# A causal mask added by TensorE's products, maximum and subtraction from the banks, and steps moved between phases

## The reference

```python
h = patches @ W + b + pos ;  h = concat([cls_tok, h])              # 32 images x 26 tokens
h = h + attn1(layernorm(h))                                       # causal
y = layernorm(h)
    # attn2: rms_norm(y) * norm1_w, qkv, rope, then
    scores = where(tril, q @ k.T / sqrt(64), finfo.min); attn = softmax(scores)
    x2 = y + attn @ v @ w_out
    # experts: two of 16 by top_k of softmax(rms_norm(x2) @ w_router)
    out = x2 + sum_e combine[:, e] * ((silu(gate) * up) @ w_down[e])
return h + out
```

## Time and profile before

| | us |
|---|---|
| median of 3 runs | 337.66 (336.48 to 338.42) |
| profiled execution | 340.81 |
| its span, first to last instruction | 338.9 |
| busy: TensorE, weight loads | 274.5, 232.9 |
| busy: VectorE, GpSimd, ScalarE | 149.4, 123.8, 91.5 |
| mean granted clock of TensorE | 0.934 |

### The profile page before, as it was taken

The page is one execution under the profiler, slowest core; times in us unless marked ns, Lnnn a source line. Parts: engine busy times, 40 slices in busy tenths (PEclk is TensorE's granted clock), DMA queues, the critical chain, the costliest instruction groups (busy, mean ns, idle before and its releaser), DMA issues.

```text
span 338.9 us, 5708 instructions
## 1 busy us (share of the span) xinstructions
PE 274.5 (81%) x1917; PEld 232.9 (69%) x1917; DVE 149.4 (44%) x347; ACT 91.5 (27%) x248; POOL 123.8 (37%) x138
## 2 busy tenths in 40 slices
PE   1999889979889999698999779803899999999900
PEld 0988779868768889487998669703677776777600
DVE  0143845764744568733867843570022222222204
ACT  1016640204532216512100532100233333333200
POOL 5030002573001291011794056063334523666640
PEclk9999999959999999999999999755899999999965
DMA  7301992004500007000000000392111596222226
GB/s 297 156 2 43 390 314 71 2 0 140 140 0 21 0 2 186 2 5 17 1 2 0 3 1 21 96 343 76 37 35 39 163 281 169 72 70 58 62 72 219
DMA packets 16641, 30.56 MB, mean 90 GB/s; under 512 B 6500, under 2 KB 10820, under 8 KB 15780
## 3 DMA queue, kind: packets, MB, share of 16 engines
q1 hardware_dynamic: 11140, 20.43, 20.1%
q0 software_dynamic: 2720, 4.55, 4.8%
q10 hardware_dynamic: 2752, 5.18, 4.5%
HBM read 26.07 MB, written 4.09 MB: 89 GB/s over the span
## 4 chain that ended last, share of the span: by engine, by line
PE 31%; DVE 21%; issue 16%; POOL 14%; DMA 11%; ACT 6%; SPq 0%; POOLq 0%; DVEq 0%; ACTq 0%
PE bank L1228 8%; POOL front L596 4%; POOL slots L580 4%; DMA experts<-wgu 4%; POOL parts L602 3%; PE bank L1244 3%; PE bank L1286 2%; PE bank L1333 2%; POOL rstd_a L516 2%; PE bank L1112 2%; DVE experts L835 2%; DMA front<-fw 2%; DVE experts L951 2%; DMA front<-moe_in,probs_by_key 2%; DVE experts L829 2%
## 5 line engine op out<-in xcount | busy, mean ns | idle before, releaser
L1100 PE MATMUL bank<-constants 128*128 128x96 f32 x376 | 48.4, 289 | 15.3 <-DMA slots<-slot_contents,slot_index 15.3
L1100 PEld LDWEIGHTS bank<-constants 128*128 128x128 f32 x376 | 47.1, 205 | 16.0 <-DMA slots<-slot_contents,slot_index 15.5
L1333 PE MATMUL bank<-experts,probs_by_key 96*128 x152 | 52.3, 487 | 0.6 <-ACT probs_by_key L758 0.6
L596 POOL DMA_INDIRECT front<-moe_in,probs_by_key x27 | 25.9, 958 | 44.8 <-DMA front<-moe_in,probs_by_key 40.1
L1333 PEld LDWEIGHTS bank<-experts,probs_by_key 96*128 96x128 f32 x152 | 27.3, 190 | 16.0 <-issue 0.8
L1053 DVE TENSOR_TENSOR probs_by_key<-bank,probs_by_key 128x384 f32<-128x384 f32 x19 | 10.6, 558 | 59.7 <-PE bank L1333 59.7
L1228 PE MATMUL bank<-experts,front 96*96 96x208 f32 x160 | 31.8, 360 | 2.4 <-DVE experts L912 2.4
L516 POOL TENSOR_TENSOR rstd_a<-variance_a,constants 128x2 f32<-128x2 f32 x12 | 8.3, 694 | 69.6 <-DVE variance_a L806 62.2
L1228 PEld LDWEIGHTS bank<-experts,front 96*96 96x96 f32 x160 | 27.8, 174 | 5.5 <-DVE experts L912 2.8
L580 POOL DMA_INDIRECT slots<-slot_contents,slot_index x16 | 16.1, 1009 | 28.9 <-DVE slot_index L1013 24.6
L912 DVE TENSOR_TENSOR experts<-bank,constants 96x416 f32<-96x416 f32 x40 | 21.1, 580 | 10.8 <-POOL experts L555 10.1
(11 more groups left out here) (167 smaller groups left out, 442.3 us busy)
## 6 DMA issues: line engine op xcount, KB each, us to landing
experts<-wgu SPq DMA_DIRECT2D x6, 768.0 KB, 8.9
experts<-wgu SPq DMA_DIRECT2D x12, 288.0 KB, 8.8
patches<-xp SPq DMA_DIRECT2D x6, 384.0 KB, 3.8
experts<-wdn SPq DMA_DIRECT2D x1, 2304.0 KB, 16.4
experts<-wdn ACTq DMA_DIRECT2D x8, 288.0 KB, 4.3
front<-fw SPq DMA_DIRECT2D x1, 1840.0 KB, 9.5
experts<-wgu ACTq DMA_DIRECT2D x4, 288.0 KB, 6.6
front<-fw SPq DMA_DIRECT2D x1, 776.0 KB, 8.8
```

Of the source, the lines that this page charges most:

```text
L596: pool.indirect_dma_start(xy[:, j * D:j * D + D], None, moe_in, bass.IndirectOffsetOnAxis(entry[:, j * 3 + 1:j * 3 + 2].bitcast(I32), 0)). ...
L1100: mm(bank[:, 0:96], eye, eye[:, 0:96], start=True, stop=True)
L1333: last = mm(ps[2 * half][:, 0:FF], xT[:, 128 * k:128 * k + 128], big[0:C, bass.ds(e * (4 * FF) + (GU0 + 2 * FF * k + FF * half), FF)], sta ...
```

## The change

- The mask is written into the bank by products in front of the scores: `mask_keys` with start=True, the scores then add (start=False). In a4 one product per image and tile (8 a group, 32x32 identity by 312 columns of mask), in b3 one per tile (26 x 104 one-hot by 312 columns).
- VectorE takes maximum and subtraction per tile straight from the bank; the masked addition goes.
- In a8 both variances are worked out from the same moments, GpSimd takes one power over 4 columns, VectorE writes u from hB directly, and then zB. ScalarE's squares of a8 go, with their waits, which VectorE gets.
- GpSimd's four memsets for B0 go from b1 to a3 of group 1 (three) and a6 of group 0 (one). Those for B3 stay.
- `place(0)` goes from behind phase 4 to behind phase 5, `scatter(0)` from behind phase 4 to behind phase 7.
- Fillers: a4 of group 0 from 9 to 5, b1 from (18, 0, 18, 0) to (9, 0, 10, 0), b7 of group 2 from 4 to 0.
- From tile 13 on, GpSimd gathers tile j + 8 only if it is used.

```diff
             def rstd(g, n):
-                s = (0, 0, 0, 1)[n]
+                s, cols = ((0, GT), (0, 2 * GT), None, (1, GT))[n]
                 pool.wait_ge(ve_ready[n], g + 1)
-                pool.tensor_tensor(rs[s][:, :], ve[s][:, :], const("neghalf"), ALU.pow).then_inc(rs_ready[n], 1)
+                pool.tensor_tensor(rs[s][:, 0:cols], ve[s][:, 0:cols], const("neghalf")[:, 0:cols], ALU.pow)\
+                    .then_inc(rs_ready[n], 1)
...
+            def a3(g):
+                if g == 1:
+                    pool.memset(B[0].p2[:, :, :, :, S:32], 0.0)
+                    pool.wait_ge(patch_done, 4)
+                    pool.memset(B[0].ot2a, 0.0)
+                    pool.memset(B[0].ot2b, 0.0)
+            def a6(g):
+                if g == 0:
+                    pool.wait_ge(o_done, 1)
+                    pool.memset(B[0].pbd, 0.0).then_inc(pads_set, 1)
             def a8(g):
                 w = A[g]
                 rstd(g, 1)
-                rstd(g, 2)
...
-            stages([a1, a2, nothing, nothing, nothing, nothing, nothing, a8],
-                   [b1, b2, nothing, nothing, nothing, b6, nothing, nothing], {4: scatter})
+            stages([a1, a2, a3, nothing, nothing, a6, nothing, a8],
+                   [b1, b2, nothing, nothing, nothing, b6, nothing, nothing], {7: scatter})
...
                 if j + AHEAD < STEPS:
-                    pool.wait_ge(gathered, (j + AHEAD) * 16)
-                    gather(j + AHEAD)
+                    if j < FEWEST:
+                        pool.wait_ge(gathered, (j + AHEAD) * 16)
+                        gather(j + AHEAD)
+                    else:
+                        with pool.If(used >= j + AHEAD):
+                            pool.wait_ge(gathered, (j + AHEAD) * 16)
+                            gather(j + AHEAD)
...
             def layer_stats(g, n, src, ready):
...
+                last = dve.tensor_scalar(ve[0][:, 0:GT], mom[:, :, 1], LN_EPS, None, ALU.add)
+                if n:
+                    last = dve.tensor_scalar(ve[0][:, GT:2 * GT], mom[:, :, 1], 1.0 + RMS_EPS, RMS_EPS * LN_EPS,
+                                             ALU.mult, ALU.add)
...
                 for t in range(GT):
                     dve.wait_ge(s_done[n], g * GT + (t + 1))
-                    bank = w.ps[(1 if n == 0 else 0) + t]
-                    dve.tensor_tensor(s3[:, 12 * t:12 * t + 12, :],
-                                      bank[0:rows, 0:12 * S].rearrange("p (h k) -> p h k", h=12),
-                                      mask.unsqueeze(1).to_broadcast([rows, 12, S]), ALU.add).then_inc(sm_ready[n], 1)
-                dve.wait_ge(sm_ready[n], g * GT + GT)
-                dve.tensor_reduce(mx[w.s][0:rows, :], s3, AX.X, ALU.max).then_inc(max_ready[n], 1)
-                dve.wait_ge(max_ready[n], g + 1)
-                dve.tensor_tensor(s3, s3, mx[w.s][0:rows, :].unsqueeze(2).to_broadcast([rows, NR, S]),
-                                  ALU.subtract).then_inc(sub_ready[n], 1)
+                    dve.tensor_reduce(mx[w.s][0:rows, 12 * t:12 * t + 12], banks[t], AX.X, ALU.max)\
+                       .then_inc(max_ready[n], 1)
+                for t in range(GT):
+                    dve.wait_ge(max_ready[n], g * GT + (t + 1))
+                    last = dve.tensor_tensor(s3[:, 12 * t:12 * t + 12, :], banks[t],
+                                             mx[w.s][0:rows, 12 * t:12 * t + 12].unsqueeze(2).to_broadcast([rows, 12, S]),
+                                             ALU.subtract)
+                last.then_inc(sub_ready[n], 1)
...
                 layer_stats(g, 1, w.hB, h1_ready)
-                normalise(g, 1, w.hB, w.zB)
-                mean_square(g, 2)
-                for t in range(GT):
-                    last = dve.tensor_scalar(w.u[:, t, :], w.zB[:, t, :], rs[0][:, t:t + 1], None, ALU.mult)
-                last.then_inc(u_ready[0], 1)
+                if g >= 2:
+                    dve.wait_ge(tokens_out[g % 2], 16 * IPT)
+                    dve.wait_ge(mt_done, g - 1)
+                normalise(w.hB, w.u, GT, u_ready[0])
+                normalise(w.hB, w.zB, 0, z_ready[1])
...
-                   {1: choose, 4: place})
+                   {1: choose, 5: place})
...
+            def mask_keys(bank, rows, queries, at):
+                mm(bank[rows, 0:12 * S].rearrange("p (h k) -> p h k", h=12), queries,
+                   const("mask1", queries.shape[0]).unsqueeze(1).to_broadcast([queries.shape[0], 12, S]),
+                   start=True, stop=False, tile_position=at)
             def a4(g):
                 pe.wait_ge(q_ready, g * 2 + 2)
                 if g == 0:
-                    keep_busy(w.ps[1], 9)
+                    pe.wait_ge(consts_in, 16)
+                    keep_busy(w.ps[1], 5)
+                for t in range(GT):
+                    for i in range(IPT):
+                        mask_keys(w.ps[1 + t], slice(32 * i, 32 * i + 32), eye[0:32, 0:32], (0, 32 * i))
                 pe.wait_ge(kbd_ready, g + 1)
...
-                keep_busy(w.ps[0], (18, 0, 18, 0)[g])
+                keep_busy(w.ps[0], (9, 0, 10, 0)[g])
...
                 for t in range(GT):
+                    mask_keys(w.ps[t], slice(0, 104), const("same_query", S), None)
...
-                keep_busy(w.ps[1], (7, 7, 4, 11)[g])
+                keep_busy(w.ps[1], (7, 7, 0, 11)[g])
```

More of the change, by code:

```diff
@@ L809, in normalise @@
+                last.then_inc(ve_ready[n], 1)
                 dve.wait_ge(rs_ready[n], g + 1)
+            def normalise(src, to, first, ready):
                 for t in range(GT):
-                    last = dve.tensor_scalar(to[:, t, :], src[:, t, :], mom[:, t, 0:1], rs[0][:, t:t + 1],
+                    last = dve.tensor_scalar(to[:, t, :], src[:, t, :], mom[:, t, 0:1], rs[0][:, first + t:first + t + 1],
                                              ALU.subtract, ALU.mult)
-                last.then_inc(z_ready[n], 1)
@@ L815, in mean_square @@
-            def mean_square(g, n):
-                s = n - 2
-                dve.wait_ge(sq_ready[s], g * GT + GT)
-                dve.tensor_scalar(ve[s][:, :], ms[s][:, :], 1.0 / D, RMS_EPS, ALU.mult, ALU.add)\
-                   .then_inc(ve_ready[n], 1)
-                dve.wait_ge(rs_ready[n], g + 1)
+                last.then_inc(ready, 1)
             def softmax(g, n, w, rows):
-                mask = const("mask1" if n == 0 else "mask2", rows)
                 s3 = w.s3
+                banks = [w.ps[(1 if n == 0 else 0) + t][0:rows, 0:12 * S].rearrange("p (h k) -> p h k", h=12)
+                         for t in range(GT)]
@@ L860, in a1 @@
                 layer_stats(g, 0, w.h, h_ready)
-                normalise(g, 0, w.h, w.z)
+                normalise(w.h, w.z, 0, z_ready[0])
             def a3(g):
@@ L1246, in b3 @@
                                       w.kbd2[:, e, IPT * t + i].rearrange("p g k -> p (g k)"),
-                                      start=(e == 0), stop=(e == 1))
+                                      start=False, stop=(i == IPT - 1 and e == 1))
                     last.then_inc(s_done[1], 1)
@@ L1411, in table_of_constants @@
     put("mask1", np.where(key <= q[:, None], 0.0, MASKED))
-    put("mask2", np.where(key <= (row[:104] % S)[:, None], 0.0, MASKED))
+    put("same_query", np.arange(S)[:, None] == (row[:104] % S)[None, :])
     put("head_of_row", row[:C, None] // HD1 == np.arange(HC))
```

44 lines of the change are left out of this document (15 added, 29 removed).

## The result

The kernel after takes 322.9 us (median, 320.9 to 324.2); before takes 337.6 (336.5 to 338.4). The ratio is 0.956, 95% interval 0.950 to 0.962: 14.7 us less, where 14.5 were forecast. Run again beside the experiments, it took 324.0 (ratio 0.960, 0.955 to 0.966). Some executions run at a lower clock and more than 1.5% above the fastest of their kernel; ratios and intervals leave them out, the medians of the tables hold them.

The account below looks back on a forecast made before the run. No engine bounds the whole: the tower's chain goes from engine to engine, and TensorE works without a gap in the expert stage. The terms sum to -14.5 us, 337.66 to 323.2; the range is 319 to 328.5.

Parts of the forecast that it names:

- Memsets, -5.5: Around 62 us: moving GpSimd's B0 memsets removes TensorE's 2.44 us wait and half clock over 16 passes; -5.5 us.
- Squares, -2.05 twice and -0.75: Stage A phase 8: u comes earlier for groups 0 and 3, -2.05 us each; ScalarE's copies for B1 earlier, -0.75.
- the rival that the clock would fall there: Phase 8 of stage A: fewer fillers let the clock fall, half clock through round 1; +21 us, 344; chance 0.04.
- Masks: Mask products on TensorE before the scores: 1.2 us for A's 16 passes, 1.05 us for B's 4 passes.
- The rival of strips that don't overlap: A's mask passes cost 4.2 us instead of 1.2 in all four A groups: +12 us, 335.2; chance 0.05.
- Softmax and rounds 1, 2, +0.22 each: Second and third LEAD/FOLLOW pairs: B's mask +1.05, softmax gains -0.63 and -0.2; each round +0.22 us.
- Round 0, -0.8: First LEAD/FOLLOW pair: TensorE-bound, fewer filler passes but added masks; A1's transposes start at 43.8 instead of 44.63, -0.8 us.
- z held, +0.65: Last pair: B3's memsets may hold VectorE's second z product, TensorE then waiting 1.3 us; half taken, +0.65.
- Round 3, -3.5: Last pair, up to u of B3: mask and softmax -0.4, place(0) moved -1.75, scatters moved -1.45; rounded -3.5 us.
- c and d: Last pair: place(0) behind B3's copies, -1.75 us; eight scatters no longer hold B2's rstd, -1.45 at u of B3.
- Scatters, +1.5: After u of B3: all 16 scatters stand behind B3's hsum add, taking 21.1 us from u against 19.6 before; +1.5.
- Gathers, -2.46: Expert stage end: without unused gathers the last scatter starts 0.2 us after its y, at 322.9 instead of 325.36; -2.46.

Follow-up runs that it names:

- the second profile: Profile of the kernel after run once more, unchanged, as the base for runs with one part undone; median 324.0 us, ratio 0.960 to before.
- the first profile: Profile of the kernel after in its first measurement, with a start 1.1 us shorter than in before; median 322.9 us, ratio 0.956 to before.
- the last experiment: Kernel after with masks put in TensorE's gaps, B3's memsets later, three scatters earlier, B3's filler cut; 320.2 us, ratio 0.947 to before.

## Why the prediction was right, step by step

The forecast was 323.2, the median 322.9 and 324.0. Nearly all mechanisms held; several sizes did not, and the errors cancel: that 323.2 is within 0.3 us of the first median is luck. The rows came from an execution of before 3.15 us above its median, and the differences were carried to the median whole.

- **Memsets, -5.5.** Right in place and kind. 5.5 between the two profiles: the 40 rope passes of B0 run from 63.07 to 75.75 us in before and in 7.20 us in after. 3.9 when undone. The wait (2.4, or 2.0) came each time; the half clock behind it cost 2.8 in the profile I had and 0 to 1.7 in three others. I priced one execution's clock as the kernel's. The profiled execution of before has a mean clock of 0.934 and took 340.81; in the runs beside the experiments the ten of before with 0.949 or more took 334.8 to 336.9, those with 0.937 to 0.942 mostly 337 to 339. So the executions of before differ with their clock; whether it falls in this stretch the unprofiled ones don't show. It would also be why the profiles differ by more (16.4 us in span) than the medians (14.7 and 14.6).
- **Squares, -2.05 twice and -0.75.** Measured between the kernels -2.0 at A8(0) (3.2 less 1.2 of round 0), -2.1 at A8(3) and -1.0 up to the rope of B1, for the copies for B1. Another -0.4 lies between u of A0 and the rope of B0 (63.07 against 59.43 us, -3.6, where u is -3.2), and comes back when the squares are undone: the prediction had A8(1) at nothing, since other work covers it, but there TensorE waited 0.18 us for ScalarE's copies behind the squares; the power over four columns took 1.02 us, inside the bounds 0.71 to 1.2 and near the 0.96 taken. Halving the fillers cost nothing, and the rival that the clock would fall there didn't come: TensorE waits 0.46 and 1.12 us, the latter twice my estimate of 0.5. With the squares undone TensorE waited 2.45 us, and it fell.
- **Masks.** A 1.25 us where 1.2 was taken, B 1.22 where I had 1.05; I left out the fill of the pipeline. The rival of strips that don't overlap (4.2) is gone.
- **Softmax and rounds 1, 2, +0.22 each.** The undoing gives +0.16 and +0.17.
- **Round 0, -0.8.** Too small: 1.2 to 1.3 in four comparisons. I added whole rows, 10.8 us from the first filler to the transposes of A1, where groups overlap at their ends: it took 10.3 (33.08 to 43.41 in the second profile).
- **z held, +0.65.** It was held: 1.04 us, nearer to the 1.3. The last product starts 0.06 us behind the first memset; the first z got through. The Trainium skill (SBUF — State Buffer, SBUF: two separate sides) gives the ports to the one that starts first, for the whole instruction. The trace agrees on who wins (the memset, 0.06 us ahead), but the product waits not for the first memset (0.30 us) but for all four that stand in GpSimd's queue, 3.83 us.
- **Round 3, -3.5.** -4.0 in the first profile once z is taken out (u of A3 to u of B3, -2.96 less 1.04). 3.65 of it are c and d. The -0.4 of the mask there is 1.9 when undone, of which 1.1 is a gap that it fills; no step of mine had that.
- **Scatters, +1.5.** Mis-sized: +0.45. 16 scatters took 20.2 us in the first profile and 20.5 in the second, instead of 21.6. Of this 0.5 was a drag that hardly came: behind the first (1.53) the pitch was 1.26 us throughout in the first profile, and in the second three were longer (1.34 to 1.40). The rest is the 0.95 us from the list's release (196.08) to the first scatter (197.03) in before, which I kept; in after the lists had long been there and it started 0.18 us behind GpSimd's own step.
- **Gathers, -2.46.** -3.2 between the profiles, 0.2 when undone: an accident of phase in before, rightly read, wrongly taken as fixed.

## What to carry to other kernels

Undo each part of a joined change in the finished kernel and do it alone in the old one: here the part in the title was worth 0 alone and 3 to 4 us in company, since other parts had made a gap that it filled. Price a wait as certain and a half clock behind it as a chance, and shorten a filler only together with the wait that it covers. When a queue's step is moved, ask what is behind it in its new place at the new time: half of a pair of moves cost 6 us. Compare the mean clocks of many executions before one profile is taken for the kernel.

## What the runs showed of the hardware

- The same 16 passes behind a wait of 2.44 us ran once at half clock throughout (5.86 us), twice at half for part (4.74, waits 2.45 and 1.97), once at full (3.05). Waits of 1.30 us (0.50 at 177 to 181 us) and 1.50 us (0.50 at 38 to 43 us) between stretches of work were followed by it too; waits of 1.41 and 1.87 us in before (for u of A3 and for the copies for B3) were not, the clock being 1.00 there.
- From the end of the last list scatter to the first gather, which waits for the lists to land and to be read back, 4.7 to 6.6 us passed in the 14 profiles, with the same transfers: (237.37 - 232.63) in before, (220.38 - 213.76) in the last experiment. With the half clock it is the largest difference between executions that the traces show; against the second profile of after it took 0.5 us of that experiment's gain.
- GpSimd's power: 0.70 us over 2 columns, 1.02 over 4.
